# New orders for all engines, with the cosine stacks transposed by DMA

## What is computed

```python
def _L0_attn_ref(x, Wq, Wk, Wv, Wo, bo):
    Q, K, V = _l2norm(heads(Wq)), _l2norm(heads(Wk)), heads(Wv)
    cos_sim = jnp.clip(jnp.einsum('bhtd,bhsd->bhts', Q, K), -0.999, 0.999)
    W = jnp.power(jnp.maximum(1.0 - jnp.arccos(cos_sim) / jnp.pi, EPS), 16.0)
    W = W / (jnp.sum(W, axis=-1, keepdims=True) + EPS)
    ...
def _L0_ffn_ref(x, W_qkv, b_qkv, W_gate, b_gate, W_experts, b_experts):
    attn = jax.nn.softmax(jnp.einsum('bqhd,bkhd->bhqk', q, k) / jnp.sqrt(hd), axis=-1)
    gate = jax.nn.softmax(x @ W_gate + b_gate, axis=-1)
    top_g, top_i = jax.lax.top_k(gate, TOP_K)
    ...
def _L1_ffn_ref(x, w_gate, w_up, w_down):
    h = jax.nn.silu(fp4_linear(x, w_gate)) * fp4_linear(x, w_up)
    return fp4_linear(h, w_down)

xn = _layernorm(x)
x = x + _L0_attn_ref(xn, ...) + _L0_ffn_ref(xn, ...)
xn = _layernorm(x)
x = x + _L1_attn_ref(xn, ...) + _L1_ffn_ref(xn, ...)
```

## Time and profile before

| | |
|---|---|
| three runs | 1963.91, 1973.51 (median), 1976.74 us |
| the profiled execution | 1969.34 us |
| its span, first to last instruction | 1967.5 us |
| VectorE busy | 1766.3 us, 90% |
| ScalarE busy | 1765.2 us, 90% |
| TensorE busy | 1486.0 us, 76% |
| GpSimd busy | 1182.2 us, 60% |
| DMA queue of SyncE, share of 16 engines | 1.8% |

### The profile page before, as it was taken

How to read it: one execution, slowest core, us unless ns; L and a number is a source line. 1 busy time by engine, 2 the same in 40 slices (tenths; PEclk the granted TensorE clock), 3 DMA queues, 4 the chain that set the end, 5 groups by cost and what they waited for, 6 DMA issues and landing times.

```text
span 1967.5 us, 38505 instructions
## 1 busy us (share of the span) xinstructions
PE 1486.0 (76%) x12022; PEld 752.9 (38%) x12022; DVE 1766.3 (90%) x4009; ACT 1765.2 (90%) x1856; POOL 1182.2 (60%) x540
## 2 busy tenths in 40 slices
PE   2667787777777877777787787878777787777766
PEld 1223434333443433344343344343334434333433
DVE  5779999999999999999999999999999999999864
ACT  1299999999999999999999999899999999999893
POOL 1566666666666566566656666665667666665640
PEclk9578889889889888888978888897888889888776
DMA  1000000000000000000000000000000000000000
GB/s 42 3 4 1 6 1 6 5 6 6 6 3 3 6 5 6 6 6 0 6 6 5 6 5 6 0 6 6 5 6 5 6 0 6 6 5 6 4 3 6
DMA packets 21058, 11.19 MB, mean 6 GB/s; under 512 B 1431, under 2 KB 20953, under 8 KB 20956
## 3 DMA queue, kind: packets, MB, share of 16 engines
q1 hardware_dynamic: 20956, 10.20, 1.8%
HBM read 6.00 MB, written 4.19 MB: 5 GB/s over the span
## 4 chain that ended last, share of the span: by engine, by line
DVE 34%; ACT 24%; issue 22%; PE 16%; DVEq 1%; POOL 1%; SPq 0%; ACTq 0%; DMA 0%; POOLq 0%
ACT curve L578 13%; DVE nmax L880 6%; DVE curve L870 5%; ACT root L578 4%; PE psM L1037 3%; PE psM L1045 3%; DVE curve L874 3%; DVE acc L854 2%; PE psM L1190 1%; DVE stkT L866 1%; DVE xn L776 1%; ACT prob L578 1%; ACT L609 1%; PE psS L1095 1%; DVE h L454 1%
## 5 line engine op out<-in xcount | busy, mean ns | idle before, releaser
L530 POOL TENSOR_TENSOR root<-curve 128x2048 f32<-128x2048 f32 x128 | 478.7, 3740 | 453.1 <-DVE curve L874 453.1
L578 ACT ACTIVATE curve<-curve 128x2048 f32<-128x2048 f32 x384 | 718.8, 1907 | 5.5 <-POOL curve L533 2.2
L578 ACT ACTIVATE root<-root 128x2048 f32<-128x2048 f32 x256 | 484.6, 1906 | 0.0
L533 POOL TENSOR_TENSOR curve<-curve,root 128x2048 f32<-128x2048 f32 x64 | 354.5, 5562 | 64.4 <-ACT root L578 64.4
L578 ACT ACTIVATE prob<-psS 128x1024 f32<-128x1024 f32 x256 | 256.7, 1029 | 66.1 <-PE psS L1097 63.9
L874 DVE TENSOR_SCALAR curve<-psS 128x1024 f32<-128x1024 f32 x256 | 308.4, 1216 | 2.7 <-PE psS L1068 2.7
L880 DVE TENSOR_REDUCE nmax<-psS 128x4 f32<-128x1024 f32 x256 | 303.0, 1215 | 1.0 <-PE psS L1077 1.0
L566 POOL TENSOR_TENSOR stk<-qk,stk 128x512 f16<-128x512 f32 x128 | 147.8, 1164 | 76.9 <-ACT stk L578 76.6
L1045 PE MATMUL psM<-we,xnT 128*128 128x512 f32 x256 | 168.8, 747 | 0.0
L870 DVE TENSOR_TENSOR curve<-curve,root 128x2048 f32<-128x2048 f32 x64 | 162.0, 2531 | 6.1 <-ACT root L578 6.1
L1221 PE MATMUL psV<-curve,vc 128*32 128x256 f32 x2048 | 140.8, 406 | 29.8 <-ACT curve L578 25.9
(11 more groups left out here) (194 smaller groups left out, 2800.2 us busy)
## 6 DMA issues: line engine op xcount, KB each, us to landing
xt<-in_L_attn_x SPq DMA_DIRECT2D x32, 128.0 KB, 2.1
out<-yo SPq DMA_DIRECT2D x32, 128.0 KB, 1.8
we<-in_L_ffn_W_experts SPq DMA_DIRECT2D x1, 512.0 KB
...
curve<-in_L_ffn_W_qkv SPq DMA_DIRECT2D x1, 128.0 KB
```

Of the source, the lines that this page charges most:

```text
L530: nc.gpsimd.tensor_tensor(root[:, two], curve[:, p, two], curve[:, p, two], ALU.mult).then_inc(s_sq, 1)
L533: nc.gpsimd.tensor_tensor(curve[:, p, two], curve[:, p, two], root[:, two], ALU.mult).then_inc(s_half[0], 1)
L578: return nc.scalar.activation(out, in_, func, **kw)
```

## The change

- The orders of all engines are new: nearly each entry has another place, and some have another lag because the border between two steps has moved.
- The cosine kinds of `stackT` leave TensorE and VectorE. SyncE issues two DMA transposes for each kind, SBUF to SBUF, 128x512 f16 each, once the stack is ready and the cosine scores of the batch before are done. `c` waits for all of q's and k's.
- GpSimd's `sq` and `mul` are two instructions of 128x1024 each in place of one of 128x2048.
- The copies of `xqT` (128x256) and `p1T` (128x384) out of PSUM move from ScalarE to VectorE.

```diff
     "sync": [
-        ("load", 0, 1), ("down", 0, -2),
+        ("load", 0, 1), ("stackT", 2, 1), ("stackT", 3, 1), ("down", 0, -2),
     ],
...
@@ sync
+                if stage == "stackT" and KINDS[arg] < 2:
+
+                    kind = KINDS[arg]
+                    sp.wait_ge(s_stk, due(s_stk, b, arg + 1))
+                    sp.wait_ge(s_c, due(s_c, b - 1))
+                    sp.sem_inc(s_cosI, 1)
+                    for j in range(NT):
+                        sp.dma_start_transpose(
+                            stkT[:, kind, :, j * P:(j + 1) * P],
+                            stk[:, kind, j * HEADS:(j + 1) * HEADS, :, :].rearrange("p h s d -> p (h s d)")).then_inc(s_cosT[kind], 16)
...
@@ gpsimd
-                two = slice(arg * 2 * UC, (arg + 1) * 2 * UC)
+                one, other = (slice((2 * arg + k) * UC, (2 * arg + k + 1) * UC) for k in range(2))
                 if stage == "sq":
...
-                    nc.gpsimd.tensor_tensor(root[:, two], curve[:, p, two], curve[:, p, two], ALU.mult).then_inc(s_sq, 1)
+                    nc.gpsimd.tensor_tensor(root[:, one], curve[:, p, one], curve[:, p, one], ALU.mult)
+                    nc.gpsimd.tensor_tensor(root[:, other], curve[:, p, other], curve[:, p, other], ALU.mult).then_inc(s_sq, 1)
...
-                    nc.gpsimd.tensor_tensor(curve[:, p, two], curve[:, p, two], root[:, two], ALU.mult).then_inc(s_half[0], 1)
+                    nc.gpsimd.tensor_tensor(curve[:, p, one], curve[:, p, one], root[:, one], ALU.mult)
+                    nc.gpsimd.tensor_tensor(curve[:, p, other], curve[:, p, other], root[:, other], ALU.mult).then_inc(s_half[0], 1)
...
@@ gpsimd and scalar, "high"
+                    if kind < 2:
+                        act.wait_ge(s_cosT[kind], due(s_cosT[kind], b - 1))
+                    else:
+                        act.wait_ge(s_stkTp, due(s_stkTp, b - 1, arg + 1))
...
@@ scalar loses and vector gains
-                    activate(p1T[:, :, :].rearrange("p k q -> p (k q)"), bank[:, 0:3 * P], ACT.Copy).then_inc(s_p1T, 1)
...
-                    activate(xqT[:, :], bank[:, 0:T], ACT.Copy).then_inc(s_xqT, 1)
...
+                    nc.vector.tensor_copy(xqT[:, :], bank[:, 0:T]).then_inc(s_xqT, 1)
...
+                    nc.vector.tensor_copy(p1T[:, :, :].rearrange("p k q -> p (k q)"), bank[:, 0:3 * P]).then_inc(s_p1T, 1)
...
@@ tensor, "c"
-                    pe.wait_ge(s_stkT, due(s_stkT, b))
+                    for kind in range(2):
+                        pe.wait_ge(s_cosT[kind], due(s_cosT[kind], b))
```

More of the change, by code:

```diff
@@ L66 @@
-        ("hT", 1, -2), ("c", 0, 1), ("gu", 0, -1), ("m", 5, 1), ("m", 6, 1), ("gu", 1, -1), ("c", 1, 1), ("m", 7, 1),
-        ("down", 0, -2),
+        ("c", 3, 0), ("c", 4, 0), ("experts", 0, 0), ("c", 5, 0), ("pvw", 0, -1), ("maxT", 0, 0), ("experts", 1, 0),
+        ("e", 0, 0), ("c", 6, 0), ("pvw", 1, -1), ("s1", 0, -2), ("pvw", 2, -1), ("c", 7, 0), ("e", 1, 0),
+        ("xnT", 0, 1), ("pvw", 3, -1), ("proj", 0, 1), ("finc", 0, -1), ("proj", 1, 1), ("p1T", 0, -2), ("e", 2, 0),
[5 rows of a table added]
     ],
     "vector": [
-        ("c", 2, 0), ("s1", 0, -2), ("finf", 0, -1), ("quanth", 1, -2), ("c", 3, 0), ("c", 4, 0), ("quanth", 2, -2),
@@ L71 @@
[L71 to L75, removed]
@@ L81 @@
-        ("down", 0, -2),
+        ("maxT", 0, 0), ("quanth", 1, -2), ("c", 3, 0), ("experts", 0, 0), ("c", 4, 0), ("c", 5, 0),
+        ("quanth", 2, -2), ("ln0", 0, 1), ("experts", 1, 0), ("c", 6, 0), ("rstd0", 0, 1), ("quanth", 3, -2),
+        ("xnT", 0, 1), ("c", 7, 0), ("s1", 0, -2), ("quanth", 4, -2), ("proj", 0, 1), ("finc", 0, -1),
+        ("quanth", 5, -2), ("quanth", 6, -2), ("proj", 1, 1), ("p1T", 0, -2), ("gmax", 0, 1), ("quanth", 7, -2),
+        ("finf", 0, -1), ("norm", 0, 1), ("ocT", 0, -1), ("choose", 0, 1), ("o1", 0, -2), ("wo", 0, -1),
@@ new lines @@
+        ("ln1", 0, -1), ("quanth", 8, -2), ("rstd1", 0, -1), ("xn1T", 0, -1), ("quantx", 0, -1), ("newton", 0, 1),
+        ("quantx", 1, -1), ("choose", 1, 1), ("quantx", 2, -1), ("choose", 2, 1), ("stackT", 0, 1), ("quantx", 3, -1),
+        ("quantx", 4, -1), ("quantx", 5, -1), ("choose", 3, 1), ("stackT", 1, 1), ("quantx", 6, -1), ("choose", 4, 1),
+        ("quantx", 7, -1), ("m", 0, 1), ("quantx", 8, -1), ("m", 1, 1), ("m", 2, 1), ("xqT", 0, -1), ("m", 3, 1),
+        ("m", 4, 1), ("mul", 1, 0), ("m", 5, 1), ("hmul", 0, -1), ("c", 0, 1), ("m", 6, 1), ("p1", 0, -1),
@@ L82 @@
+        ("mul", 3, 0), ("c", 1, 1), ("hmul", 1, -1), ("m", 7, 1), ("c", 2, 1), ("down", 0, -2), ("quanth", 0, -1),
     ],
     "scalar": [
[L84 to L91, removed]
+        ("wexp", 0, -1), ("wln", 2, -1), ("maxT", 0, 0), ("wexp", 1, -1), ("wexp", 2, -1), ("ln0", 0, 1),
[3 rows of a table added]
@@ L92 @@
+        ("e", 6, 0), ("xn1T", 0, -1), ("e", 7, 0), ("high", 2, 1), ("table", 1, 0), ("high", 3, 1), ("sigm", 0, 0),
+        ("hT", 0, -2), ("sigm", 1, 0), ("hT", 1, -2), ("sigm", 2, 0), ("arctan", 0, 0), ("gu", 0, -1), ("sigm", 3, 0),
+        ("arctan", 1, 0), ("p1", 0, -1), ("arctan", 2, 0), ("gu", 1, -1), ("arctan", 3, 0), ("table", 0, 0),
+        ("wln", 0, 0), ("wln", 1, 0),
     ],
     "gpsimd": [
-        ("fadd", 0, -1), ("sq", 2, 0), ("sq", 3, 0), ("norm", 0, 1), ("high", 0, 1), ("high", 1, 1), ("stack", 0, 1),
@@ L371, in build @@
             READ[("hT", j, 0)] = (s_hT, j + 1)
-        for kind in range(4):
-            READ[("stackT", kind, 0)] = (s_stkT, kind + 1)
+        for arg in range(2):
+            READ[("stackT", arg, 0)] = (s_stkT, arg + 1)
         def bank_read(stage, arg, use, t, uses=MISC):
@@ L856, in run @@
                                                        ALU.add).then_inc(s_moe, 1)
-                if stage == "stackT":
+                if stage == "stackT" and KINDS[arg] >= 2:
                     kind = KINDS[arg]
@@ L993, in run @@
                     nc.vector.tensor_copy(ocT[:, :], bank[:, 0:T]).then_inc(s_ocT, 1)
+                if stage == "xqT":
+                    bank, k = misc_bank(stage, 0, 0)
+                    dve.wait_ge(s_xqTp, due(s_xqTp, b))
+                    dve.wait_ge(s_gup, due(s_gup, b - 1))
+                    nc.vector.tensor_copy(xqT[:, :], bank[:, 0:T]).then_inc(s_xqT, 1)
+                if stage == "p1T":
+                    bank, k = misc_bank(stage, 0, 0)
+                    dve.wait_ge(s_p1Tp, due(s_p1Tp, b))
+                    dve.wait_ge(s_o1p, due(s_o1p, b - 1))
+                    nc.vector.tensor_copy(p1T[:, :, :].rearrange("p k q -> p (k q)"), bank[:, 0:3 * P]).then_inc(s_p1T, 1)
             steps(dve, ORDER["vector"], run)
```

43 lines of the change are left out of this document (14 added, 29 removed), and 11 rows, old and new, of the table ORDER.

## The result

The changed kernel is slower: 2122.85 us in the median of four runs against 1974.61, a ratio of 1.076 (95% interval 1.073 to 1.079). Forecast were 1930 us and a range of 1890 to 1985. The time is near the 2095 us of the second rival, but, as the profile shows, not by its mechanism.

What follows compares the result with a forecast made beforehand. VectorE and ScalarE, level and nearly full, were taken to bound the kernel. Terms -0.4 - 1.3 - 0.3 - 0.3 + 0.9 gave -1.4 us a step, 30 times, less 3 us of gain for fill: 1930 us, range 1890 to 1985.

Steps and rivals of the forecast that it cites:

- the second rival: DMA transposes land late at the first c, stalling TensorE, VectorE and ScalarE: +5.5 us a step, 2095 us, chance 0.13.
- What bounds the kernel: Whole step: VectorE and ScalarE, each busy 90% of the span, are level and nearly full; step of 58.97 us.
- VectorE's own work: VectorE: two stack copies go (1.36 us), copies of xqT (0.42) and p1T (0.55) come; net -0.4 us a step.
- ScalarE's 0.86 us: ScalarE: two copies leave it, which lets VectorE's savings through and adds none of its own.
- The order, waits: VectorE: new order hides 1.3 of 1.84 us waiting for the second projection and 0.3 of 0.58 for the second rstd.
- GpSimd's products in two: VectorE beside GpSimd: halves shorten gl and the two products, a third of 0.94 us, -0.3 us a step (0 to -0.9).
- the rule of the Trainium skill: SBUF: a GpSimd instruction and a VectorE one with two SBUF inputs exclude each other; by it alone -0.5 us, not -0.3.
- New waits: ScalarE and TensorE around hT and the two gu places: 0.45 us each, +0.9 us a step.
- the 4 us that was named as a sign of error: ScalarE: waiting for TensorE more than 4 us a step would make the prediction wrong.
- The DMA term: SyncE's four transposes before the first c: 11.3 us free, no stall under 2.8 us each, one after another; taken as 0.
- Fill: First batch, uncovered transposes and engines filling by a new order: +3 us once, between 0 and 10.
- the wait of c: TensorE's c waiting for stkT: no wait above 0.3 us was expected if the DMA term held.

Runs made afterwards that it cites:

- the inverse: Kernel before the change, choose 3 (ge) moved behind stackT 3 and choose 4 (comb) behind m 4, beside GpSimd's two 128x2048 products: 2098.5 us, ratio 1.064.

## Why the prediction was wrong

- **What bounds the kernel: right in part.** In the changed kernel it is VectorE alone: busy time and time went nearly one for one (107 us busy and 104 of the profiled execution with two entries moved, 131 and 130 in the inverse), while ScalarE had time to spare. In the kernel before a shorter VectorE gained less (28 us less busy with GpSimd's products cut, 16 us of time), which fits two engines that are level. 58.97 us was one long step; the mean is 57.91.
- **VectorE's own work: right.** Copies of 41.0 us went, 17.6 and 13.1 came: -0.3 us a step, forecast -0.4.
- **ScalarE's 0.86 us: right to count it at nothing.** No run shows that it let VectorE's savings through; alone, in other places, the two copies cost 1.8 us a step.
- **The order, waits: right for the two that it named.** VectorE's wait for the second projection fell from 1.84 to 0.45 us a step, and that for rstd vanished. But part of it came back elsewhere: acc (an expert's product, from TensorE) waits 1.18 us a step where it waited 0.14, and the cosine scores (L879) 0.45. In all VectorE idles 0.45 us a step less, where the prediction, with its new waits, had 0.7. Over ten steps, the kernel before first:

```profile
DVE acc L854 <- PE psM L1045: 1.4, 5, 0.4
```

```profile
DVE acc L862 <- PE psM L1060: 11.8, 12, 2.1
DVE qk L805 <- PE psM L1052: 4.5, 8, 0.7
...
ACT h L593 <- PE psM L1206: 47.4, 21, 3.2
```

- **GpSimd's products in two, -0.3 us: here it failed.** The step asked what the halves would do to the waits that the old order had. It never asked which of VectorE's instructions the new order puts beside GpSimd's, halved or not, and so the sum has no term for them. That was +5 us a step (VectorE's busy time rose by 4.72 us with 0.3 less work of its own): with GpSimd's products cut down 132 us went, with three entries moved 145. The halves' own saving did not show either: gl takes 0.76 us in the mean where it took 0.56, and the halves alone in the kernel before gave nothing. The sentence that the trace does not agree with the rule of the Trainium skill was a wrong reading of the earlier trace rows. The row 1033.59 11.07 holds two instructions (x2). The first, at the 4.52 us that is its least, ended at 1038.1; VectorE's product waited 0.4 us for it and ended at 1040.27, and the second waited in turn. The rule, which the step set aside, was the one that decides. Nor was best the proof of it: best is a copy with a single SBUF operand. It did wait (0.85 us in the mean), so instructions with two are not the only ones to ask about.
- **New waits, +0.9: wrong place.** VectorE waited 0.18 us a step at hmul. ScalarE waited 4.7 us a step for gu, above the 4 us that was named as a sign of error. In the changed kernel it had that time to spare: with three entries moved the loss was gone and this wait was not (59.0 us in all). It came to count only once VectorE was freed.
- **The DMA term, 0: right.** 2.5 us each, under 2.8, and 1.5 us of waiting in all. They do overlap: four take 6.5 us and not 10.
- **Fill, +3: mis-sized, +22 us.** With GpSimd's products cut it is 26 us, with six entries and gu moved 27; why the start and the end are longer stays open.
- **Rival 2** had nearly the measured time, 2095 us, and the wrong mechanism. A near number shows nothing; the wait of c, which it named as its sign, was not there.
